# Input tiles by one three-dimensional transfer each, and another order of TensorE's work, in the first two of four image layers

## The chip, the core and the metric

The program runs on one core of one Trainium2 chip. The metric is the device time of one execution in microseconds (us), as the median of several runs. A profile of one execution is shown beside it: TensorE (PE, with its weight loads as PEld), VectorE (DVE), ScalarE (ACT), GpSimd (POOL), and SyncE (SP), which only issues transfers here. A "q" behind an engine's name stands for its queue of issued transfers and of semaphore work.

## What is computed

Sixteen images of 224 x 224 pixels with 32 channels pass four layers. Each adds a function of its group-normalised input to the input. Only layers 0 and 1 are touched by the change:

```python
# layer 0: a shift by an offset that the image's own mean decides
mean_feat = jnp.mean(x, axis=(1, 2))
offsets = jnp.clip(mean_feat @ W + b, 0, 28).astype(jnp.int32)      # dy, dx
x = x + shifted(group_norm(x), dy, dx)                              # zeros come in at the top and left
# layer 1: a 3x3 convolution of signs
y = conv(sign(group_norm(x)), sum_of_signs(W)) + b.sum(axis=0)
x = x + y
# layers 2 and 3: a low-frequency product in a cosine/Fourier basis, plus x @ W.T + b, then relu, added to x
```

## The kernel before

The program has three phases. The first, `shift_conv_forward`, does layers 0 and 1 and the forward spectrum that layer 2 needs. The later phases (names that begin with B_ and C_) do layers 2 and 3 and are not touched.

**Tiles.** An image lies in SBUF as [128 partitions, 12544]; partition 32 i + c holds channel c of every fourth image row (i = 0 to 3). It comes from DRAM in 16 input tiles of [128, 896] f32, each of which holds 28 pixels of 32 channels (3584 bytes in one piece in DRAM) for 128 image rows. VectorE transposes a tile in blocks of 32 x 32 and so turns rows of pixels into rows of channels. Each image is read twice: once as it is (`load_x`, transposed at L805 in `turn_x` straight into `image`), and once shifted by its offset (`load_shifted`, transposed at L815 in `add_shifted` into `moved`, masked, and added to the image at L830). So 32 tiles are read per image. They pass a ring of four buffers `rin`: SyncE issues tile n only when VectorE has turned tile n - 4 (`tile_turned`).

**A tile's load.** `load` (L355 to L361) makes four transfers, one for each i. Each takes 32 pieces of 3584 bytes, 4 image rows apart, to 32 partitions, and adds 16 to the buffer's semaphore when it has landed; VectorE waits for 64.

**The order of the work** is written out by hand. Each engine runs `body(b, ...)` for b = -1 to 15, and each body has 16 slots s = 0 to 15. Body b does at once the convolution of image b (14 units of two double lines, one in each slot 0 to 13), the shifted add of image b + 1, and the plain load and the sums of image b + 2; in its first slots it also finishes the spectrum of image b - 1. `X_BY` and `S_BY` say which tiles fall in which slot: by slot 4 a body has turned 13 of its 32 tiles, by slot 9 it has turned all plain tiles and 10 shifted ones, and the last shifted one is in slot 12.

**TensorE in a slot:** `conv` (L470 to L477, unit s), two spectrum steps in the first slots (L522, L533), in odd slots from 3 `forward_cols`, called the column product here (L509, eight f32 matmuls, product p = (s - 3) / 2 from 0 to 6), and `turn_back` (L498, the transposition of unit s - 1, which waits for VectorE's L838). ScalarE copies what `turn_back` made (`copy_back`, L612) into one of two buffers `tout`, and waits for the column product that read it before; `turn_back` waits for earlier copies.

**The small products** `statistics` (L436): i = 1 and 2 make the group mean and variance of image b + 2 (slots 12 and 13), i = 4 the mean that centres image b + 1 (slot 13), and i = 3, the offset average, multiplies the normalised mean of image b + 2 with the layer's weights (`wsc`, L780). VectorE waits for the offset average at L783 in slot 15, writes the offsets (L792) and signals `off_ready`. SyncE waits for that (L399) before the first shifted tile of the next body, after two plain tiles; everything else in its queue stands behind. In the kernel before, TensorE makes the offset average of image b + 2 in slot 0 of the next body, behind the first unit of its convolution.

**Stores.** ScalarE's queue stores each finished image to `x2s` in seven pieces of 896 KB (L617), SyncE's the spectrum in eight pieces of 32 KB (L379). At the start SyncE fills a padded copy `xpad` of image 0: 14 stores of zeros with 29 rows each (L351), and one copy of 64 rows (L353).

Of the kernel before, what the change touches and what calls it, by code (L numbers as in the profile page):

```python
# [26 lines left out]
SIZE = 224  # L27
C = 32
P = 128
HR = SIZE // 2  # L30
QG = P // C
# [105 lines left out]
def shift_conv_forward(nc, NB, x, w1, b1, w0, b0, con, statm, xpad, x2s, spec):  # L137
# [4 lines left out]
    with Semaphores(nc) as sems, ctx:  # L142
        def sb(name, shape, dt=f32):
            return ctx.enter_context(nc.sbuf_tensor("A_" + name, shape, dt))

        def sem(name):
            return sems.new("A_" + name)

        CHQ = 28
        TILES = 16  # L150
# [4 lines left out]
        RING = 4  # L155
# [8 lines left out]
        rin = [sb(f"rin{i}", [P, CHQ * C]) for i in range(RING)]  # L164
# [48 lines left out]
        in_full = [sem(f"in_full{i}") for i in range(RING)]  # L213
# [40 lines left out]
        def x_tiles(s):  # L254

            return range(X_BY[s - 1] if s else 0, X_BY[s])

        def s_tiles(s):

            return range(S_BY[s - 1] if s else 0, S_BY[s])  # L260

        def x_at(k):

            s = [k < by for by in X_BY].index(True)
            return k + (S_BY[s - 1] if s else 0)

        def s_at(k, has_x):

            return k + (X_BY[[k < by for by in S_BY].index(True)] if has_x else 0)

        def tile_no(b, at):

            return TILES + 2 * TILES * (b + 1) + at

        def tile_loaded(b, at):

            return 64 * (2 * TILES // RING * b + 3 * TILES // RING + at // RING + 1)

        def stat_tiles(s):

# [28 lines left out]
        def ring_base(b):  # L309

            if isinstance(b, int) and b == 0:
                return 0
            return 36 * b - 8
# [33 lines left out]
        @block.sync  # L347
        def _(sp):
            sp.wait_ge(setup, 1)
            for g in range(SIZE * C // BANK):  # L350
                sp.dma_start(xpad[0:29].rearrange("r q c -> r (q c)")[:, g * BANK:(g + 1) * BANK],  # L351
                             zrow).then_inc(pad_done, 16)
            sp.dma_start(xpad[29:29 + P].rearrange("r q c -> r (q c)"),  # L353
                         x[0, 0:P].rearrange("r q c -> r (q c)")).then_inc(pad_done, 16)

            def load(flat, k, slot):
                rows = flat.rearrange("(l f) c -> l (f c)", l=32)
                for i in range(QG):
                    first = i * SIZE + (k % 8) * CHQ
                    sp.dma_start(rin[slot][32 * i:32 * i + 32, :],  # L360
                                 rows[:, first * C:(first + CHQ) * C]).then_inc(in_full[slot], 16)  # L361

            def load_x(b, k, slot):
                load(x_pix[bass.ds(b * (SIZE * SIZE) + (k // 8) * (QG * SECOND * SIZE), P * SIZE), :], k, slot)

            def load_shifted(b, k, slot, back):
                if isinstance(b, int) and b == 0 and k < 8:
                    load(pad_pix[bass.ds(29 * SIZE - back, P * SIZE), :], k, slot)
                else:
                    load(x_pix[bass.ds(b * (SIZE * SIZE) + (k // 8) * (QG * SECOND * SIZE) - back, P * SIZE), :], k, slot)  # L370

            def store_spec(b):
                sp.wait_ge(spec_sb, b + 1)
                sp.sem_inc(off_seen, 1)
                plane = spec[bass.ds(b, 1)].rearrange("o p f -> (o p) f")
                planes = plane.rearrange("(g e c) (m y) -> g e m c y", g=4, e=2, m=16)
                for e in range(2):
                    for g in range(4):
                        sp.dma_start(planes[g, e],  # L379
                                     specout[64 * e + 16 * g:64 * e + 16 * g + 16, :].rearrange("m (c y) -> m c y", y=MODES)  # L380
                                     ).then_inc(spec_stored, 16)

            for k in range(TILES):
                if k >= RING:
                    sp.wait_ge(tile_turned, k - RING + 1)
                load_x(0, k, k % RING)
            sp.wait_ge(pad_done, 16 * (SIZE * C // BANK + 1))

            def body(b, has_x, has_tail):
                back = None  # L390
                for s in range(SLOTS):
                    for k in x_tiles(s) if has_x else ():
                        sp.wait_ge(tile_turned, tile_no(b, x_at(k)) - RING + 1)
                        sp.sem_inc(off_seen, 1)
                        load_x(b + 2, k, x_at(k) % RING)
                    for k in s_tiles(s):
                        if k == 0:
                            sp.wait_ge(off_ready, b + 2)
                            sp.sem_inc(off_seen, 1)  # L399
                            dy = sp.value_load(offi[0:1, 0:1], min_val=0, max_val=MAXOFF)  # L400
                            dx = sp.value_load(offi[0:1, 1:2], min_val=0, max_val=MAXOFF)
                            back = dy * SIZE + dx
                            sp.sem_inc(off_taken, 1)
                        sp.wait_ge(tile_turned, tile_no(b, s_at(k, has_x)) - RING + 1)
                        sp.sem_inc(off_seen, 1)
                        load_shifted(b + 1, k, s_at(k, has_x) % RING, back)
                    if has_tail and s == 6:
                        store_spec(b - 1)

            body(-1, True, False)  # L410
            body(0, True, False)
            with sp.Fori(0, (NB - 4) // 3) as i:
                for k in range(3):
                    body(3 * i + 1 + k, True, True)
            body(NB - 3, True, True)
            body(NB - 2, False, True)
            store_spec(NB - 2)
            store_spec(NB - 1)
            sp.wait_ge(spec_stored, 8 * 16 * NB)

        @block.tensor
        def _(pe):
# [16 lines left out]
            def statistics(b, i):  # L439
                k = average_no(b, i)  # L440
                done = b if i == 4 else b - 1
                if not isinstance(done, int) or done > 0:
                    pe.wait_ge(spec_sb, done)
                if i == 1:
                    average(k, [(mps[:, 2:3], con["k_pair"][:], mv[:, 0:1]), (mps[:, 3:4], con["k_same"][:], mv[:, 0:1])])
                elif i == 2:
                    average(k, [(mps[:, 4:5], con["k_pair"][:], sm[:, 2:3])])
                elif i == 3:
                    average(k, [(mps[:, 6:8], ones[0:C, :], wsc[:])])
                else:  # L450
                    average(k, [(mps[:, 8:9], con["k_pair"][:], sm[:, 8:9])])
# [94 lines left out]
            def body(b, q, has_v, has_s, has_x, has_tail):  # L546
                for s in range(SLOTS):
                    if has_v and s < UNITS:
                        conv(b, s)
                    if has_v and has_s and s == 0:  # L550
                        statistics(b, 3)
                    if has_tail and s < 5:
                        spectrum(b - 1, 2 * s, ring_base(b))
                    if has_v and s >= 3 and s % 2 == 1:
                        forward_cols(b, q, (s - 3) // 2)
                    if has_v and 1 <= s <= UNITS:
                        turn_back(b, q, s - 1)
                    if has_tail and s < 4:
                        spectrum(b - 1, 2 * s + 1, ring_base(b))
                    if has_x and s in (12, 13):  # L560
                        statistics(b + 1, s - 11)
                    if has_s and s == 13:
                        statistics(b, 4)

            body(-1, 2, False, True, True, False)
            body(0, 0, True, True, True, False)
# [137 lines left out]
        def _(dve):  # L704
            at = {"base": 0, "n": 0}
# [26 lines left out]
            for i in range(QG):  # L732
                rows = slice(32 * i, 32 * i + 32)
# [68 lines left out]
            def turn_x(q, k, slot, loaded):  # L802
                t, ch = divmod(k, 8)
                dve.wait_ge(in_full[slot], loaded)
                nc.vector.transpose(turned_view(image[q], SECOND * t, ch * CHQ, CHQ),  # L805
                                    flat_view(rin[slot][:, :])).then_inc(tile_turned, 1)
# [75 lines left out]
            for k in range(TILES):  # L882
                if k >= 8:
                    dve.wait_ge(junk_done, junk_x(0, ("square", k - 8)) + 1)
                turn_x(0, k, k % RING, 64 * (k // RING + 1))
                if k == 0:
                    guess(0, 0)
            for i in (0, 1, 2, 4, 3):
# [958 lines left out]
```

## Time and profile before

| | us |
|---|---|
| median of 3 runs | 3735.57 (3716.77 to 3765.04) |
| the profiled execution's device time | 3730.91 |
| its span, first to last instruction | 3729.1 |
| TensorE busy | 3021.7 (81%) |
| VectorE busy | 2734.8 (73%) |
| ScalarE busy | 1510.7 (41%) |
| DMA, mean over the span | 217 GB/s |

The profile is of one execution. A busy share is a mean over stages with different limits, so the stretches of the first phase are read apart below. "Idle before" is the idle time of an engine just before an instruction, and the name behind the arrow is what ended it. The DMA share is the mean busy share of the core's 16 DMA engines.

### The profile page before, as it was taken

Reading aid. Unit: us, or ns where it says so; the run is one execution under the profiler, and the core shown is the slowest. Engines: PE = TensorE matmul, PEld = TensorE weight load, DVE = VectorE, ACT = ScalarE, POOL = GpSimd, SP = SyncE. Lnnn points to the kernel's source line nnn. Section 1 sums busy time; section 2 is a strip of 40 time slices with the busy share of each in tenths; the row PEclk is TensorE's granted clock in tenths of the full one; section 3 lists DMA queues with packets and bytes.
Section 4 is the critical chain, followed back from the end, with each engine's and each line's share of the span. In section 5 each row is a group of like instructions: output and inputs, shape, how many; then the busy total and the mean of one; then the engine's idle time right before and its main releaser. Section 6 shows DMA issues by size and latency. Waiting matters only on the chain. (4 is left out here: it accounts for less than half of the span.)

```text
span 3729.1 us, 58608 instructions
## 1 busy us (share of the span) xinstructions
PE 3021.7 (81%) x17264; PEld 1399.1 (38%) x17264; DVE 2734.8 (73%) x3908; ACT 1510.7 (41%) x2728; POOL 38.0 (1%) x35
## 2 busy tenths in 40 slices
PE   0188888888888888898937988888898827999997
PEld 0033343333444334344426433333333306444443
DVE  3888777778787777887523677776867643999998
ACT  3466765566665566665443322222222223000000
POOL 0000000000000000000010000000000010000000
PEclk9988887788787778889976999999999867999998
DMA  4677655667565666665364746556465355999998
GB/s 147 174 219 213 199 183 170 192 196 216 175 192 180 190 197 201 195 194 166 122 142 144 287 197 241 227 214 256 186 261 205 144 118 149 341 389 392 377 382 302
DMA packets 272198, 808.67 MB, mean 217 GB/s; under 512 B 85466, under 2 KB 119774, under 8 KB 261108
## 3 DMA queue, kind: packets, MB, share of 16 engines
q1 hardware_dynamic: 212948, 488.15, 41.2%
q10 hardware_dynamic: 58368, 316.72, 21.9%
q8 instruction: 115, 1.88, 0.2%
q0 software_dynamic: 608, 0.63, 0.1%
q14 instruction: 159, 1.30, 0.1%
HBM read 479.39 MB, written 329.56 MB: 217 GB/s over the span
## 5 line engine op out<-in xcount | busy, mean ns | idle before, releaser
L1425 ACT ACTIVATE B_junk<-B_im,B_nk 128x896 bf16<-128x896 f32 x224 | 232.8, 1039 | 718.0 <-DVE B_im L1483 583.2
L470 PE MATMUL A_cps<-A_sign,A_cfull 128*128 128x448 bf16 x1344 | 421.9, 399 | 12.2 <-issue 8.9
L1676 PE MATMUL C_ring<-C_im,C_wnorm 128*128 128x448 f32 x896 | 387.7, 571 | 23.2 <-DVE C_ubuf L1733 17.7
L498 PE MATMUL A_aps<-a_k_ident,A_image 128*112 128x128 f32 x1792 | 289.0, 308 | 134.3 <-DVE A_image L838 112.4
L1371 PE MATMUL B_ring<-B_im,B_wnorm 128*128 128x448 f32 x896 | 385.1, 571 | 7.0 <-DVE B_wnorm L1454 4.8
L612 ACT ACTIVATE A_tout<-A_aps 112x512 f32<-112x512 f32 x448 | 248.3, 591 | 350.1 <-PE A_aps L498 349.6
L475 PE MATMUL A_cps<-A_sign,A_cedge 32*32 32x448 bf16 x1344 | 379.7, 392 | 0.0
L477 PE MATMUL A_cps<-A_sign,A_cedge 32*32 32x448 bf16 x1344 | 379.2, 392 | 0.2 <-issue 0.2
L1343 PE MATMUL B_ring<-B_rout,b_k_rowf 128*64 128x512 f32 x896 | 279.4, 707 | 118.4 <-DVE B_rout L1476 118.4
L838 DVE SCALAR_TENSOR_TENSOR A_image<-A_cps,A_cbias,A_image 128x896 f32<-128x896 f32 x224 | 256.7, 1146 | 156.6 <-PE A_cps L470 153.3
L1483 DVE SCALAR_TENSOR_TENSOR B_im<-B_ring,B_im 128x896 f32<-128x896 f32 x224 | 239.0, 1084 | 175.4 <-PE B_ring L1381 173.8
L815 DVE STREAM_TRANSPOSE A_moved<-A_rin 128x896 f32<-128x896 f32 x256 | 283.3, 1107 | 86.9 <-DMA A_rin<-in_x 71.5
L805 DVE STREAM_TRANSPOSE A_image<-A_rin 128x896 f32<-128x896 f32 x256 | 276.9, 1100 | 88.4 <-DMA A_rin<-in_x 72.2
L498 PEld LDWEIGHTS A_aps<-a_k_ident,A_image 128*112 128x112 f32 x1792 | 239.0, 187 | 254.5 <-issue 189.4
L509 PE MATMUL A_vps<-A_tout,a_k_dctj 112*32 112x512 f32 x896 | 263.4, 717 | 14.9 <-ACT A_tout L612 14.7
L830 DVE SCALAR_TENSOR_TENSOR A_image<-A_moved,A_lin,A_image 128x896 f32<-128x896 f32 (+1 forms) x256 | 265.0, 1035 | 9.1
L1742 DVE STREAM_TRANSPOSE C_rout<-C_im 128x2048 f32<-128x2048 f32 (+1 forms) x128 | 259.2, 2027 | 4.8 <-DMA out<-C_rout 3.2
L1476 DVE STREAM_TRANSPOSE B_rout<-B_im 128x2048 f32<-128x2048 f32 (+1 forms) x128 | 256.5, 2025 | 0.0
L594 ACT ACTIVATE A_junk<-A_image 128x896 bf16<-128x896 f32 (+1 forms) x256 | 219.6, 858 | 79.5 <-DVE A_image L805 69.1
L1371 PEld LDWEIGHTS B_ring<-B_im,B_wnorm 128*128 128x128 f32 x896 | 160.5, 189 | 236.2 <-issue 209.7
L600 ACT ACTIVATE A_junk<-A_image,A_nx 128x896 bf16<-128x896 f32 (+1 forms) x256 | 242.9, 949 | 8.5
L1748 DVE SCALAR_TENSOR_TENSOR C_im<-C_ring,C_im 128x896 f32<-128x896 f32 x224 | 235.0, 1069 | 14.6 <-PE C_ring L1686 12.6
(196 smaller groups left out, 3472.1 us busy)
## 6 DMA issues: line engine op xcount, KB each, us to landing
A_rin<-in_x SPq DMA_DIRECT2D x2016, 112.0 KB, 2.4
x2s<-A_image ACTq DMA_DIRECT2D x112, 896.0 KB, 4.8
B_im<-x2s SPq DMA_DIRECT2D x112, 896.0 KB, 9.6
x3s<-B_im ACTq DMA_DIRECT2D x112, 896.0 KB
C_im<-x3s SPq DMA_DIRECT2D x112, 896.0 KB, 11.9
out<-C_rout ACTq DMA_DIRECT2D x192, 256.0 KB
out<-C_rout ACTq DMA_DIRECT2D x192, 192.0 KB
out<-C_rout ACTq DMA_DIRECT2D x64, 128.0 KB
```

The source lines that it names most:

```text
L470: return nc.tensor.matmul(banks[:, s, 0:LPN], cfull[:, tap, :], lines(n, s, slice(0, P), 0, tap), start=(tap == 0), stop=(tap == 2), skip_ ...
L475: nc.tensor.matmul(banks[bottom, s_top, 0:LPN], cedge[top, tap, :], lines(n, s_top, top, -1, tap), start=False, stop=False, skip_group_che ...
L477: nc.tensor.matmul(banks[top, s_bottom, 0:LPN], cedge[bottom, tap, :], lines(n, s_bottom, bottom, 1, tap), start=False, stop=False, skip_g ...
L498: last = nc.tensor.transpose(aps[side][0:HR, l * P:(l + 1) * P], image[q][:, first:first + 2 * HR].rearrange("p (j s) -> p s j", s=2)[:, l ...
L509: last = nc.tensor.matmul(vps[32 * g:32 * g + 32, :], con["k_dctj"][:, half, :], tout[G % OUTS][:, half, :], start=(half == 0), stop=(half ...
L805: nc.vector.transpose(turned_view(image[q], SECOND * t, ch * CHQ, CHQ), flat_view(rin[slot][:, :])).then_inc(tile_turned, 1)
L815: nc.vector.transpose(moved[:, :].rearrange("p (l q s) -> p q l s", q=CHQ, s=2), flat_view(rin[at_tile % RING][:, :])).then_inc(tile_turne ...
L830: nc.vector.scalar_tensor_tensor(out=dst, in0=m[:, lo:16, :], scalar=lin[:, 0:1], in1=dst, op0=ALU.mult, op1=ALU.add, accum_out=addsum[:, ...
L1343: last = nc.tensor.matmul(bank[64 * side:64 * side + 64, hq, :], con["k_rowf"][:, t, :], rout[p % 2][:, t, q0:q0 + BANK], start=(t == 0), ...
L1371: nc.tensor.matmul(slot(par, ("add", e))[:, lane % 2, 0:2 * SIZE], wnorm[par][:], im[par][:, EVN * e:EVN * (e + 1)].rearrange("p (m s) -> ...
L1676: nc.tensor.matmul(slot(add_place(e))[:, lane % 2, 0:2 * SIZE], wnorm[par][:], im[par][:, EVN * e:EVN * (e + 1)].rearrange("p (m s) -> p s ...
L1742: nc.vector.transpose(flat_view(rout[p][:, 0:wide * C]), turned_view(im[par], SECOND * t, p * PIECEQ, wide)).then_inc(rout_full, 1)
```

## The change

Three edits, all in `shift_conv_forward`:

1. `load` makes one transfer for a tile. Its source is three-dimensional (4 by 32 by 896 elements: i outermost, then the 32 groups of four image rows, then the piece of 3584 bytes), its destination the 128 partitions. The same 128 pieces go to the same places. VectorE waits for 16 where it waited for 64.
2. In slot 13 column product 5 stands behind `turn_back` and the variance product, in place of ahead of them. Column product 6 stays in slot 15; the other five stay too.
3. The offset average of the image after next stands at the end of slot 15, ahead of the next body's first convolution, where it stood behind it.

```diff
         def tile_loaded(b, at):
 
-            return 64 * (2 * TILES // RING * b + 3 * TILES // RING + at // RING + 1)
+            return 16 * (2 * TILES // RING * b + 3 * TILES // RING + at // RING + 1)
...
             def load(flat, k, slot):
-                rows = flat.rearrange("(l f) c -> l (f c)", l=32)
-                for i in range(QG):
-                    first = i * SIZE + (k % 8) * CHQ
-                    sp.dma_start(rin[slot][32 * i:32 * i + 32, :],
-                                 rows[:, first * C:(first + CHQ) * C]).then_inc(in_full[slot], 16)
+                rows = flat.rearrange("(l i q) c -> i l (q c)", i=QG, q=SIZE)
+                first = (k % 8) * CHQ
+                sp.dma_start(rin[slot][:, :], rows[:, :, first * C:(first + CHQ) * C]).then_inc(in_full[slot], 16)
...
                 for s in range(SLOTS):
                     if has_v and s < UNITS:
                         conv(b, s)
-                    if has_v and has_s and s == 0:
-                        statistics(b, 3)
                     if has_tail and s < 5:
                         spectrum(b - 1, 2 * s, ring_base(b))
-                    if has_v and s >= 3 and s % 2 == 1:
+                    if has_v and s in (3, 5, 7, 9, 11):
                         forward_cols(b, q, (s - 3) // 2)
...
                     if has_x and s in (12, 13):
                         statistics(b + 1, s - 11)
+                    if has_v and s == 13:
+                        forward_cols(b, q, 5)
                     if has_s and s == 13:
                         statistics(b, 4)
+                    if has_v and s == 15:
+                        forward_cols(b, q, 6)
+                    if has_x and s == 15:
+                        statistics(b + 1, 3)
...
-                turn_x(0, k, k % RING, 64 * (k // RING + 1))
+                turn_x(0, k, k % RING, 16 * (k // RING + 1))
```

SyncE's instructions at the start of the program, before the change (L360 is the tile's load; a row shows the destination's shape):

```order
L351 DMA xpad<-A_image 29x512 x14
L353 DMA xpad<-in_x 64x14336
L360 DMA A_rin<-in_x 32x896 x72
L400 TENSOR_LOAD A_offi
L400 ISA x2
```

The same place with the change, where the load is L359:

```order
L351 DMA xpad<-A_image 29x512 x14
L353 DMA xpad<-in_x 64x14336
L359 DMA A_rin<-in_x 128x1x896 x18
L398 TENSOR_LOAD A_offi
L398 ISA x2
```

Where 72 transfers loaded 18 tiles, there are 18 now, each with 128 destination rows; their source pattern begins with the dimension of 4.

TensorE in slots 13 and 14 of a body in the loop, before the change, from column product 5 on (L509 column product, L498 `turn_back`, L436 small products; REGISTER_ALU rows only count for waits):

```order
L505 REGISTER_ALU
L509 MATMUL A_vps<-A_tout,a_k_dctj 32x512 x4
L491 REGISTER_ALU
L430 REGISTER_ALU
L498 MATMUL A_aps<-a_k_ident,A_image 112x128 x8
L434 REGISTER_ALU
L436 MATMUL A_wps<-A_sm,a_k_pair 128x1
L434 REGISTER_ALU
L436 MATMUL A_wps<-A_sm,a_k_pair 128x1
L491 REGISTER_ALU
L430 REGISTER_ALU
```

The same place with the change (all lines of TensorE's body are two lower):

```order
L489 REGISTER_ALU
L428 REGISTER_ALU
L496 MATMUL A_aps<-a_k_ident,A_image 112x128 x4
L428 REGISTER_ALU
L496 MATMUL A_aps<-a_k_ident,A_image 112x128 x4
L432 REGISTER_ALU
L434 MATMUL A_wps<-A_sm,a_k_pair 128x1
L507 MATMUL A_vps<-A_tout,a_k_dctj 32x512 x4
L432 REGISTER_ALU
L434 MATMUL A_wps<-A_sm,a_k_pair 128x1
```

The column product moved from ahead of `turn_back` to between the two small products.

TensorE at the seam of two bodies, before the change: the last rows of the next body's first convolution, and the offset average (A_wsc) behind them:

```order
L477 MATMUL A_cps<-A_sign,A_cedge 32x448
L470 MATMUL A_cps<-A_sign,A_cfull 128x448 x2
L434 REGISTER_ALU
L436 MATMUL A_wps<-A_wsc,A_ones 128x2
L430 ISA
L522 MATMUL A_aps<-a_k_ident,A_rowspec 64x128 x4
```

With the change it stands between column product 6 and that convolution:

```order
L502 REGISTER_ALU
L503 REGISTER_ALU
L507 MATMUL A_vps<-A_tout,a_k_dctj 32x512 x4
L432 REGISTER_ALU
L434 MATMUL A_wps<-A_wsc,A_ones 128x2
L463 ISA
L468 MATMUL A_cps<-A_sign,A_cfull 128x448 x2
```

The offset average moved ahead by one unit of the convolution.

## Rows read from the trace of the kernel before

**Rows 1.** Stretches: each engine's busy us (instructions), granted clock, DMA share, GB/s.

```profile
36.00:80.00 44.00, 0.00 (x0) 0.00 (x0) 15.65 (x16) 21.65 (x41) 0.00 (x0) 1.00 0.80 251
170.00:1725.00 1555.00, 1343.78 (x7292) 603.45 (x7292) 1220.77 (x2236) 998.68 (x1898) 0.00 (x0) 0.82 0.63 193
1725.00:1910.00 185.00, 168.68 (x1108) 84.01 (x1108) 89.83 (x171) 78.24 (x146) 0.00 (x0) 0.97 0.35 114
850.00:862.00 12.00, 12.00 (x48) 5.89 (x50) 8.51 (x19) 7.52 (x14) 0.00 (x0) 0.51 0.75 238
870.00:882.00 12.00, 12.00 (x84) 5.79 (x83) 11.22 (x15) 11.84 (x23) 0.00 (x0) 1.00 0.60 192
```

**Rows 2.** Line L783: ns min/median/max, first and last start; whom it waited for.

```profile
L783 DVE TENSOR_TENSOR A_sm<-A_wps,A_b0s x16: 158/159/160, 96.8 to 1723.7; 128x2 f32<-128x2 f32 x16
  PE A_wps L436: 68.7, 16
```

**Rows 3.** Waits from 100 to 1725 us: total us, times, longest.

```profile
PE A_aps L498 <- DVE A_image L838: 111.5, 55, 6.0
DVE A_moved L815 <- DMA A_rin<-in_x: 65.3, 79, 2.6
PE A_wps L436 <- DVEq L845: 47.9, 13, 4.0
...
DVE A_image L805 <- DMA A_rin<-in_x: 41.3, 37, 2.2
```

**Rows 4.** SyncE's queue in order of time: start, us, issues, count.

```profile
2.01 0.43 SPq L132 DMA_DIRECT2D a_k_ident<-k_ident  x1
...
7.07 24.90 SPq L351 DMA_DIRECT2D xpad<-A_image  x14
32.01 3.81 SPq L353 DMA_DIRECT2D xpad<-in_x  x1
...
664.49 39.49 SPq L360 DMA_DIRECT2D A_rin<-in_x  x64
```

**Rows 5.** Stretches of the zero stores: granted clock, DMA share, GB/s.

```profile
20.00:24.00 4.00, 1.00 0.07 26
24.00:28.00 4.00, 1.00 0.07 26
```

**Rows 6.** DMA view, 3300 to 3600 us: packets, MB, then each queue's share.

```profile
DMA packets 21974, 115.26 MB, mean 384 GB/s; under 512 B 5080, under 2 KB 5080, under 8 KB 16039
q1 hardware_dynamic: 10118, 58.58, 49.9%
q10 hardware_dynamic: 11856, 56.68, 46.0%
```

**Rows 7.** DMA view, 60 to 80 us, where only input tiles are loaded.

```profile
DMA packets 2018, 4.84 MB, mean 242 GB/s; under 512 B 670, under 2 KB 670, under 8 KB 2017
q1 hardware_dynamic: 2017, 4.83, 82.6%
A_rin<-in_x SPq DMA_DIRECT2D x44, 112.0 KB, 2.7
```

**Rows 8.** DMA view, 100 to 1800 us: the stores' queue, and issues.

```profile
q10 hardware_dynamic: 14976, 95.43, 14.9%
...
x2s<-A_image ACTq DMA_DIRECT2D x104, 896.0 KB, 4.8
```

**Rows 9.** In order of time, VectorE and TensorE at the end of one body.

```profile
819.27 1.11 DVE L815 STREAM_TRANSPOSE A_moved<-A_rin 128x896 f32<-128x896 f32 x1
...
832.74 0.16 DVE L783 TENSOR_TENSOR A_sm<-A_wps,A_b0s 128x2 f32<-128x2 f32 x1 [3.42 <-PE A_wps L436]
...
814.42 1.91 PE L509 MATMUL A_vps<-A_tout,a_k_dctj 112*32 112x512 f32 x8
...
817.43 0.28 PE L436 MATMUL A_wps<-A_sm,a_k_pair 128*128 128x1 f32 x2
821.66 0.59 PE L436 MATMUL A_wps<-A_sm,a_k_pair 128*128 128x1 f32 x2 [3.95 <-DVEq L845]
823.07 1.96 PE L498 MATMUL A_aps<-a_k_ident,A_image 128*112 128x128 f32 x8 [0.82 <-DVE A_image L838]
825.72 3.63 PE L509 MATMUL A_vps<-A_tout,a_k_dctj 112*32 112x512 f32 x8 [0.69 <-ACT A_tout L612]
```

## The prediction, made before the changed kernel ran

> **What bounds the kernel now.** The change touches only the first phase, so I looked for its period first. The offset line L783 runs once per body; its 16 starts span 96.8 to 1723.7 us [rows 2], so 15 bodies take 1626.9 us, 108.5 us each. Next I read the stretches [rows 1]. From 170 to 1725 us (14.33 bodies) TensorE is busy 1343.8 us, 93.7 per body, VectorE 1220.8 us, 85.2 per body. The DMA engines are busy 63%. So TensorE is nearest to being the bound, with 14.8 us idle per body, at a mean clock of 0.82: some stretches are granted 1.2 GHz (0.51 from 850 to 862 us), others 2.4 GHz (1.00 from 870 to 882), and the instruction counts there, 48 against 84, show that the same work takes 1.75 times as long. The waits [rows 3] say why it idles: 111.5 us for VectorE's L838, 47.9 us for the centring sum at L845. VectorE is late in turn because it waits for tiles, 65.3 + 41.3 = 106.6 us or 7.1 per body, and 68.7 us for the offset average, 4.6 per body [rows 2]. SyncE issues almost without pause: 64 transfers, which are 16 tiles, in 39.5 us, 2.47 us per tile [rows 4]. A body needs a tile every 3.4 us, but after the offset wait they are wanted faster. That is what one transfer per tile addresses.
>
> **The tile's transfer.** It takes three of four issues away, 96 per body. An issue of a 128-row transfer took 0.43 us [rows 4]; four now take 2.47 us. Even if the new one took the 1.78 us of the slowest kind (24.90 / 14) [rows 4], the issue would be cheaper. It isn't the issue that decides, but over how many of the 16 DMA engines the transfer is spread.
>
> Two kinds of rows bear on that. Transfers of 32 and 128 rows load many engines: tiles alone come at 242 GB/s with 82.6% of 16 engines busy [rows 7]. The 14 zero stores of 29 rows do not: while they queue up, the DMA share is 0.07 and the rate 26 GB/s [rows 5], so one engine in 16 (0.0625) works and 15 stand idle. They didn't spread one to an engine either: each is 29 x 2048 = 59,392 bytes, 2.3 us at 26 GB/s, and SyncE issued one every 1.78 us, so two engines would often have been busy at once. So a transfer is dealt out by its outermost dimension, only in equal parts (29 has none), and each starts on the same engine. The new transfer's destination begins with 128 and its source with 4. Equal parts of both exist for 4 engines, not for 16. No transfer in this trace has two sides with different outermost dimensions, so this step is an inference.
>
> The Trainium skill (DMA: Bandwidth & Descriptors, "Why a DMA increments its semaphore by 16 and not by 1") states it outright: the number of engines is the largest up to 16 that divides the slowest dimension of both sides, and these are the lowest-numbered ones. The trace agrees for 29 rows (share 0.07); for 4 against 128 it has no case.
>
> I take 4 engines, always the same 4. A tile is 458,752 bytes. Bounds for one busy engine: 26 GB/s [rows 5]; 384 / (16 x 0.959) = 25.0 in the last phase [rows 6]; and 242 / (16 x 0.826) = 18.3 for today's tiles, whose transfers leave an engine two pieces each [rows 7]. The new transfer leaves 32 pieces in a row on an engine, which is most like the first two, so I take 25.5 GB/s: 458,752 / (4 x 25.5) = 4.5 us per tile. The other end is 6.3 us.
>
> Per body these four engines carry:
> - 32 tiles x 4.5 = 144 us
> - their sixteenth of the image's stores: 14.9% of 1700 us for 104 stores is 2.44 us per store [rows 8], x 7 = 17 us
> - the spectrum's eight 32 KB stores, 16 KB for an engine: under 1 us, left out
>
> That makes 161 us, against 108.5 for the whole body now. The load becomes the bound.
>
> Two things come on top. First, no shifted tile can be issued before the offset is known. From the last tile's transposition at 819.3 to L783 at 832.7 are 13.4 us, of which 3.4 are the wait that edit 3 removes [rows 9]; two plain tiles (9 us) may be issued meanwhile, and the ring restarts with a landing time of some 2.7 us [rows 7]. I take 4 us per body. Second, TensorE's idle time grows from 14.8 to about 60 us per body, and stretches after its waits are granted 1.2 GHz. All its work at that clock would be about 140 us (93.7, of which 36% is slow already: 60 + 33.7 / 1.75 = 79 at full speed, x 1.75 = 139), still under 161. But work and tiles are not spread alike: slots 0 to 4 hold nine spectrum steps and only 13 tiles (58 us). At the low clock TensorE is the later one there. I take 3 us more. A body: 168 us.
>
> **The moved products** cost TensorE nothing in instructions. Edit 3 lets L783 start up to 4.6 us earlier [rows 2]; edit 2 puts column product 5 (eight L509 in 1.91 us at the high clock, 3.63 at the low one) into the 3.95 us in which TensorE waits for the centring sum [rows 9]. Its price: ScalarE's copy of unit 12 waits for this product, and so comes one `turn_back` and one small product later, 1 to 3 us. The next `turn_back` waits for VectorE until 823.1 us anyway [rows 9], so that is hidden. Both gains are worth up to 8 us per body if TensorE or VectorE is the bound, and nothing beyond the 3.4 us already counted if the tiles are.
>
> **The sum.** Bodies 0 to 13: 14 x 168 = 2352. Body -1 has no convolution and no stores: 144 + 6 = 150. Together 2502, against 1627: +875. The first 16 tiles take 44 us now [rows 1]; they become 16 x 4.5 = 72 plus 10 us for their share of the 7.3 MB of the copy to `xpad` ahead of them: +38. Body 14 loads 16 tiles, 72 + 17 us, against some 75 now: +12. The rest (last image, layers 2 and 3) has no tile in it: 0. In all +925. The profiled execution took 3730.9 us, 5 us under the median, so 3730 + 925 = 4655 us.
>
> **Rivals.**
> - *The transfer spreads over all 16 engines.* For it: the destination has 128 rows, like loads that do spread. Then most of the tile waits (7.1 per body) and of the offset wait (4.6) go; VectorE and TensorE lean on each other, so I count half: 6 us x 15 = 90, and 5 in the prologue: 3640 us, faster. It decides against my forecast as soon as a tile takes under (108.5 - 17) / 32 = 2.86 us, which is from 7 engines up. Beside it stands another rule of the Trainium skill (DMA: Bandwidth & Descriptors, "Rules for kernel authors"): many small transfers are better coalesced, and two to separate partitions are better made one of 128 partitions. Chance 0.10.
> - *Four engines, but other ones for each tile.* Then a tile lands some 6.5 us after its issue, which a ring of four, 3.4 us a tile, mostly hides; only the first tiles after the offset come late, 4 us, which eats the gain: about 3700 us, no change. Against it: the zero stores stayed on one engine. Chance 0.05.
> - *The same four, at 18.3 GB/s each.* If pieces of 3584 bytes are slow by themselves, a tile takes 6.3 us: 32 x 6.3 + 17 + 5 = 224 per body; 14 x 224 + 207 - 1627 = +1716, with +80 at both ends about 5525 us. Chance 0.07.
> - *Forecast as worked out.* Chance 0.78.
>
> **How the numbers follow.** The low end leaves out what I put on top and lets half of the stores pass beside the tiles: 14 x 153 + 144 = 2286, +659, and +40: about 4430; a little room below gives 4400. The high end takes TensorE late in the first five slots and a rate midway to the rival's (5.1 us a tile): 14 x 188 + 170 = 2802, +1175, and +70: about 4975; 5080 with room. It leaves out both fast cases (0.15) and most of the slow one. A change over 2% is about what these runs can tell: faster 0.09, same 0.05 (with a little of the first rival), slower 0.86.
>
> **What would show it.** Right: in the first phase the DMA share falls to about 0.25 plus the stores' part, the rate to some 110 to 130 GB/s; VectorE's waits for A_rin grow from 107 to over 700 us; TensorE's clock falls below 0.82; a tile's time to landing, with others queued ahead, is over 9 us; L783's 16 starts span about 2500 us. Wrong: a rate of 200 GB/s or more in that phase, or tiles landing in 3 us. L783's own wait should be nearly gone in any case.

## The result, and the profile after

| | before | with the change |
|---|---|---|
| median us | 3727.28 (4 runs) | 4640.93 (4 runs, 4636.58 to 4660.22) |
| span of the profiled execution, us | 3729.1 | 4634.8 |
| ratio | | 1.244, 95% interval 1.234 to 1.254 |

The change makes the kernel 24% slower. The forecast was 4655 us, the range 4400 to 5080. All ratios in this text are to runs of the kernel before made beside the run in question (medians 3725 to 3732 us for the experiments).

Where the time went is seen from the first transfer of the second phase in SyncE's queue. Before (start, us, issue):

```profile
1910.48 0.38 SPq L132 DMA_DIRECT2D b_k_pair<-k_pair  x1
```

With the change:

```profile
2818.78 0.37 SPq L132 DMA_DIRECT2D b_k_pair<-k_pair  x1
```

The first phase takes 908.3 us longer, the whole span 905.7. So all of it is in the phase that loads tiles.

Its period is that of the offset line, now L785 (ns min/median/max, first and last start, and below it the wait):

```profile
L785 DVE TENSOR_TENSOR A_sm<-A_wps,A_b0s x16: 151/159/161, 132.8 to 2599.4; 128x2 f32<-128x2 f32 x16
  PE A_wps L434: 7.3, 13
```

Fifteen bodies take 2466.6 us, 164.4 each, against 108.5 [rows 2]. The first of them, body -1, has no convolution and is shorter: it took 147.9 us (the second start is at 280.7), so the fourteen full bodies took 165.6 each. VectorE's wait for the offset average has nearly gone, 7.3 us for 68.7. The same stretch, with each engine's busy us, the clock, the DMA share and GB/s, and the last image behind it:

```profile
133.00:2599.00 2466.00, 1637.67 (x7277) 717.36 (x7278) 1303.87 (x2332) 1050.06 (x1963) 0.00 (x0) 0.68 0.32 128
2600.00:2785.00 185.00, 165.87 (x991) 77.60 (x990) 88.53 (x164) 67.66 (x127) 0.00 (x0) 0.87 0.27 103
```

TensorE is busy 66% of the stretch instead of 86% [rows 1], and longer for the same work, since the granted clock is 0.68 for 0.82. The DMA share is halved, 0.32 for 0.63, and that is the point: as a group the DMA engines look two thirds idle while everything waits for them. The waits of this stretch (total us, times, longest):

```profile
DVE A_moved L817 <- DMA A_rin<-in_x: 685.3, 232, 6.3
...
PE A_aps L496 <- DVE A_image L840: 577.5, 140, 12.2
DVE A_image L807 <- DMA A_rin<-in_x: 364.2, 181, 5.3
...
ACT A_tout L614 <- PE A_vps L507: 146.6, 14, 11.0
```

VectorE waits for tiles 1049.5 us, where it was 106.6 [rows 3], nearly every tile of the 480 (413 times), and TensorE waits for VectorE. The DMA view of the stretch says on how many engines the tiles run:

```profile
DMA packets 105668, 314.60 MB, mean 128 GB/s; under 512 B 31768, under 2 KB 31768, under 8 KB 105496
## 3 DMA queue, kind: packets, MB, share of 16 engines
q1 hardware_dynamic: 91384, 222.71, 23.0%
q10 hardware_dynamic: 14112, 89.92, 9.0%
```

The tiles' queue (q1) keeps 0.23 x 16 = 3.7 engines busy. The stores (q10) use 9% of all 16. If q1 is on four engines only, these are busy 92% of the time with tiles and 9% with stores, which leaves next to nothing. (It comes to 101%, so the times of packets of the two queues must overlap in part.) Two short stretches of one body, between two stores, show the same: while tiles come, the DMA share is 0.25, and around the offset nearly nothing moves (us, each engine's busy us, clock, DMA share, GB/s):

```profile
1440.00:1444.00 4.00, 3.27 (x12) 0.65 (x14) 1.34 (x8) 0.58 (x1) 0.00 (x0) 0.50 0.07 14
1446.00:1448.00 2.00, 1.14 (x6) 0.67 (x5) 1.93 (x5) 0.59 (x1) 0.00 (x0) 0.50 0.25 95
```

VectorE's tile transpositions show the rhythm (start, us, then idle time before):

```profile
1404.49 1.12 DVE L817 STREAM_TRANSPOSE A_moved<-A_rin 128x896 f32<-128x896 f32 x1 [1.21 <-DMA A_rin<-in_x]
1408.86 1.11 DVE L817 STREAM_TRANSPOSE A_moved<-A_rin 128x896 f32<-128x896 f32 x1 [2.29 <-DMA A_rin<-in_x]
1413.37 1.11 DVE L817 STREAM_TRANSPOSE A_moved<-A_rin 128x896 f32<-128x896 f32 x1 [0.33 <-DMA A_rin<-in_x]
1417.61 1.11 DVE L817 STREAM_TRANSPOSE A_moved<-A_rin 128x896 f32<-128x896 f32 x1 [2.16 <-DMA A_rin<-in_x]
1424.13 1.11 DVE L817 STREAM_TRANSPOSE A_moved<-A_rin 128x896 f32<-128x896 f32 x1 [2.85 <-DMA A_rin<-in_x]
1428.49 1.11 DVE L817 STREAM_TRANSPOSE A_moved<-A_rin 128x896 f32<-128x896 f32 x1 [2.29 <-DMA A_rin<-in_x]
...
1451.31 1.11 DVE L817 STREAM_TRANSPOSE A_moved<-A_rin 128x896 f32<-128x896 f32 x1 [2.48 <-DMA A_rin<-in_x]
```

A tile comes every 4.36 us (4.24 to 4.51 here), however long VectorE had idled: 458,752 bytes in 4.36 us is 105 GB/s, or 26.3 for each of four engines. Once it is 6.5 us (1417.6 to 1424.1). ScalarE issued a store at 1414.34, and the 2.2 us more are what its sixteenth, 57,344 bytes, takes at 26.3 GB/s. The last two rows are the last shifted tile of one body and the first of the next; between them stand two plain tiles, which had landed by then, and the offset.

### The profile page after: what moved, and what is told of

It reads as the page before. It is cut to its first block and busy times, and to the rows that moved or that the text cites. A ratio compares the mean times of both kernels' runs of the same rounds, so it can differ in the third digit from the quotient of the medians.

```text
span 4634.8 us, 54387 instructions
## 1 busy us (share of the span) xinstructions
PE 3326.3 (72%) x17264; PEld 1516.8 (33%) x17264; DVE 2757.5 (59%) x3908; ACT 1529.8 (33%) x2728; POOL 38.0 (1%) x35
## 5 line engine op out<-in xcount | busy, mean ns | idle before, releaser
L496 PE MATMUL A_aps<-a_k_ident,A_image 128*112 128x128 f32 x1792 | 382.3, 379 | 605.7 <-DVE A_image L840 588.2
L614 ACT ACTIVATE A_tout<-A_aps 112x512 f32<-112x512 f32 x448 | 259.2, 594 | 1053.7 <-PE A_aps L496 891.7
L496 PEld LDWEIGHTS A_aps<-a_k_ident,A_image 128*112 128x112 f32 x1792 | 304.8, 200 | 748.4 <-issue 589.3
L468 PE MATMUL A_cps<-A_sign,A_cfull 128*128 128x448 bf16 x1344 | 502.8, 466 | 5.1 <-issue 5.0
L473 PE MATMUL A_cps<-A_sign,A_cedge 32*32 32x448 bf16 x1344 | 458.3, 460 | 0.0
L475 PE MATMUL A_cps<-A_sign,A_cedge 32*32 32x448 bf16 x1344 | 457.5, 460 | 0.0
L1678 PE MATMUL C_ring<-C_im,C_wnorm 128*128 128x448 f32 x896 | 388.1, 572 | 25.7 <-DVE C_ubuf L1735 20.7
L507 PE MATMUL A_vps<-A_tout,a_k_dctj 112*32 112x512 f32 x896 | 296.6, 798 | 12.4 <-ACT A_tout L614 12.4
```

The lines of the kernel that those rows point to most:

```text
L468: return nc.tensor.matmul(banks[:, s, 0:LPN], cfull[:, tap, :], lines(n, s, slice(0, P), 0, tap), start=(tap == 0), stop=(tap == 2), skip_ ...
L473: nc.tensor.matmul(banks[bottom, s_top, 0:LPN], cedge[top, tap, :], lines(n, s_top, top, -1, tap), start=False, stop=False, skip_group_che ...
L475: nc.tensor.matmul(banks[top, s_bottom, 0:LPN], cedge[bottom, tap, :], lines(n, s_bottom, bottom, 1, tap), start=False, stop=False, skip_g ...
L496: last = nc.tensor.transpose(aps[side][0:HR, l * P:(l + 1) * P], image[q][:, first:first + 2 * HR].rearrange("p (j s) -> p s j", s=2)[:, l ...
L507: last = nc.tensor.matmul(vps[32 * g:32 * g + 32, :], con["k_dctj"][:, half, :], tout[G % OUTS][:, half, :], start=(half == 0), stop=(half ...
L1678: nc.tensor.matmul(slot(add_place(e))[:, lane % 2, 0:2 * SIZE], wnorm[par][:], im[par][:, EVN * e:EVN * (e + 1)].rearrange("p (m s) -> p s ...
```

## The experiments

The first question was whether the engines are counted by the outermost dimension. The load of the changed kernel reads `(l i q) c -> i l (q c)` with i = 4. With another number in its place the transfer is of the same kind and size, and only its outermost dimension changes.

**16 outermost.**

```diff
-                rows = flat.rearrange("(l i q) c -> i l (q c)", i=QG, q=SIZE)
+                rows = flat.rearrange("(l i q) c -> i l (q c)", i=16, q=SIZE)
```

> The changed kernel, with the source of each tile's one transfer read as 16 by 8 by 896 elements in place of 4 by 32 by 896: still one three-dimensional transfer of 128 pieces of 3584 bytes to 128 partitions, but its rows land on other partitions, so that the image is computed with its rows permuted. My theory (a transfer is dealt over as many engines as divide the outermost dimension of both sides, here 16): the load is no longer the bound, the DMA share in the first phase goes back to 0.6 or more, the 16 starts of the offset line span under 1600 us and the time is about 3640 us (3550 to 3720). Rival (a three-dimensional or a single transfer is slow as such, whatever its dimensions): about 4640 us, as the changed kernel.

Measured: 3670.7 us, ratio to before 0.982 (0.975 to 0.988). The 900 us are gone, and a little more; the DMA share from 170 to 1725 us is 0.71, and the 16 starts of the offset line span 1561 us. The DMA view from 200 to 1700 us:

```profile
q1 hardware_dynamic: 91894, 206.06, 54.6%
```

That is 8.7 engines' worth of packet time at a time, which four engines can't give. A single three-dimensional transfer is not slow as such.

**8 outermost**, the same edit with `i=8`.

> The same with 8 by 16 by 896 elements, again with the rows permuted. My theory: 8 engines, 2.25 us a tile, 32 x 2.25 + 17 = 89 us of load per body, under the 108.5 us that a body took before: about 3670 us (3600 to 3760), near the run with 16. Rival (slow as such): about 4640 us. If the time went with the reciprocal of the engines without a floor, it would be some 4000 us.

Measured: 3817.2 us, ratio 1.024 (1.019 to 1.029). It is far from 4640, as it should be, but not hidden: I expected 3670. The DMA view from 200 to 1700 us, and the offset line:

```profile
q1 hardware_dynamic: 82233, 192.46, 38.7%
q10 hardware_dynamic: 13104, 83.50, 14.0%
```

```profile
L785 DVE TENSOR_TENSOR A_sm<-A_wps,A_b0s x16: 151/159/161, 99.6 to 1804.8; 128x2 f32<-128x2 f32 x16
```

q1 moved 192.46 MB in 1500 us with 0.387 x 16 = 6.2 engines busy, 20.7 GB/s for a busy one, not 25.5. So a tile takes 458,752 / (8 x 20.7) = 2.8 us: 32 of them are 89 us, with stores 106, and with some 10 us around the offset (below) 116. The fifteen bodies took 113.7 us on average, the fourteen full ones 115.7 (the second start is at 184.6). At today's 108.5 us per body 8 engines are just too few.

**2 outermost**, the same edit with `i=2`.

> The changed kernel with the source of each tile's transfer read as 2 by 64 by 896 elements (rows permuted, as in the runs with 8 and 16). My theory: 2 engines. In the changed kernel four engines took 4.8 us of packet time each per tile (23.0% of 16 engines over 2400 us for 461 tiles), so two take 9.6 us: 32 x 9.6 + 17 + 4 = 328 us per body, and 3730 + (14 x 328 + 312 - 1627) + some 200 at both ends is about 7200 us (6800 to 7600). Rival (four engines whatever the dimension is, or a loss that does not grow with fewer engines): 4640 us.

Measured: 6780.9 us, ratio 1.819 (1.810 to 1.827). The DMA view from 200 to 1700 us:

```profile
q1 hardware_dynamic: 27736, 75.63, 12.5%
```

0.125 x 16 = 2.0: two engines, busy all the time. The time is 19 us under the range that I gave, because I took 9.6 us for a tile. Its transposition starts, where no store comes between, are 8.7 us apart:

```profile
1317.20 1.11 DVE L817 STREAM_TRANSPOSE A_moved<-A_rin 128x896 f32<-128x896 f32 x1 [5.59 <-DMA A_rin<-in_x]
1325.93 1.11 DVE L817 STREAM_TRANSPOSE A_moved<-A_rin 128x896 f32<-128x896 f32 x1 [6.66 <-DMA A_rin<-in_x]
```

That is twice the 4.36 us of four engines. 32 x 8.73 + 17 = 296 us, and the bodies took 296.9 on average ((4657.8 - 203.6) / 15) for the 328 that I had expected.

**Four transfers, each with 4 outermost.** The runs so far all have one transfer. This one has four, as the kernel before, and TensorE's new order:

```diff
 # against the kernel before; TensorE's new order is there too
-                rows = flat.rearrange("(l f) c -> l (f c)", l=32)
+                rows = flat.rearrange("(m a f) c -> a m (f c)", a=4, m=8)
...
-                                 rows[:, first * C:(first + CHQ) * C]).then_inc(in_full[slot], 16)
+                                 rows[:, :, first * C:(first + CHQ) * C]).then_inc(in_full[slot], 16)
```

> Four transfers for each tile, 32 rows each, as before the change, with TensorE's new order; but the source of each is read as 4 by 8 by 896 elements, so that its outermost dimension is 4 (rows permuted within each group of 32 partitions). My theory: each of the four runs on the same four engines, and the tile is as slow as one transfer of 4 by 32: about 4650 us (4550 to 4800). Rival (it is the single transfer with one semaphore count, or its 128 rows, that is slow): 3743 us, as with four plain transfers.

Measured: 4658.3 us, ratio 1.249 (1.244 to 1.255), with this DMA view from 200 to 1700 us:

```profile
q1 hardware_dynamic: 59293, 135.56, 23.1%
```

Four transfers on four engines are as slow as one on four, and these four tile transfers run on the same engines, or there would be more than 3.7 busy. The loss does not come from making one transfer of four. What counts is the source's outermost dimension, though the destination's is 32. In all these runs the smaller of the two sides divides the larger one; that equal parts of both are what is needed, and not the smaller side, has only the zero stores of 29 rows to show for it [rows 5], where both sides are 29.

The second question was what the moved products do.

**The load alone** (edit 1, TensorE's order of before).

```diff
 # against the changed kernel
+                    if has_v and has_s and s == 0:
+                        statistics(b, 3)
...
-                    if has_x and s == 15:
-                        statistics(b + 1, 3)
```

Column product 5 is back in its old place too.

> The kernel before with edit 1 alone: one transfer of 4 by 32 by 896 for each tile, TensorE's order as before. My theory: the load alone makes the loss, and the offset average is back behind the first convolution, so that the offset comes 3 to 5 us later in each of 15 bodies: about 4690 us (4640 to 4750). Rival (the moved products take a good part of the loss, since ScalarE waits for column product 5 in the changed kernel): 4400 us or less.

Measured: 4715.8 us, ratio 1.267 (1.261 to 1.273). It is 75 us slower than the whole change: with slow tiles the new order is worth 5 us per body. VectorE's wait at its offset line is back, 72.8 us for 7.3, 4.4 per body:

```profile
  PE A_wps L434: 72.8, 16
```

**The load and the offset average, without edit 2.**

```diff
 # against the changed kernel
-                    if has_v and s in (3, 5, 7, 9, 11):
+                    if has_v and s >= 3 and s % 2 == 1 and s < 15:
...
-                    if has_v and s == 13:
-                        forward_cols(b, q, 5)
```

> The changed kernel without edit 2: one transfer of 4 by 32 by 896 for each tile and the offset average ahead of the first convolution, but column product 5 back ahead of the transposition. My theory: all of the 75 us between the changed kernel (4641) and the load alone (4716) come from edit 3, since the offset gates the shifted tiles: 4640 us (4620 to 4665). Rival (edit 2 brings them): 4716 us.

Measured: 4647.3 us (4637.7 to 4654.7), ratio 1.246. That is the changed kernel's time. So edit 3 brings the 75 us, and edit 2 nothing measurable, with slow tiles.

**The order alone** (edits 2 and 3, four plain transfers).

```diff
 # against the kernel before
-                    if has_v and has_s and s == 0:
-                        statistics(b, 3)
...
+                    if has_v and s == 13:
+                        forward_cols(b, q, 5)
...
+                    if has_x and s == 15:
+                        statistics(b + 1, 3)
```

> The kernel before with edits 2 and 3 alone: four transfers for each tile, TensorE's new order. My theory: VectorE's wait for the offset average (4.6 us a body) goes and half of it reaches the end, some 3 us in 15 bodies, and the centring wait hides column product 5: about 3670 us (3620 to 3710). Rival (ScalarE's copy of unit 12 comes later and takes the gain back): 3720 to 3760 us, no change.

Measured: 3742.7 us, ratio 1.004 (1.001 to 1.006): no gain, but a loss of 0.4%. My theory said 3670 and falls; the rival's time is right, and its reason is not borne out by the one body looked at below. The waits of this kernel from 100 to 1725 us:

```profile
DVE A_image L842 <- PE A_cps L470: 163.6, 44, 6.8
ACT A_tout L616 <- PE A_vps L509: 109.1, 14, 9.5
```

and VectorE's wait at its offset line:

```profile
  PE A_wps L436: 3.8, 8
```

For the kernel before, the same view has this row:

```profile
DVE A_image L838 <- PE A_cps L470: 94.9, 30, 6.7
```

The offset wait fell by 64.9 us, and the wait for the convolution grew by 68.7. VectorE gets past the offset earlier and then stands before the next convolution, which TensorE reaches no sooner. So the offset wait was a place where VectorE waited for TensorE's pace, not what made the pace. ScalarE's wait for column product 5 looks large, 109.1 us, but it mostly takes the place of a wait for the transposition (294.5 us in the kernel before, 179.8 here). In one body the transposition of unit 12 ended at 823.2 us and the copy began at 825.24, 2 us later, behind the product; what comes next, the transposition of unit 13, began at 828.71 because of VectorE:

```profile
825.24 1.08 ACT L616 ACTIVATE A_tout<-A_aps 112x512 f32<-112x512 f32 x2 [5.15 <-PE A_vps L509]
```

```profile
828.71 1.13 PE L498 MATMUL A_aps<-a_k_ident,A_image 128*112 128x128 f32 x8 [1.03 <-DVE A_image L842]
```

**16 outermost with the old order.** Perhaps the offset counts once tiles are fast.

> One transfer of 16 by 8 by 896 for each tile (rows permuted), with TensorE's order of the kernel before. It tells what edits 2 and 3 are worth when tiles are fast. With the new order the same load took 3671 us. Theory (TensorE is the bound, and VectorE's wait for the offset average only becomes a wait for the convolution, as in the run of the order alone): within 0.5% of that, 3655 to 3690 us. Rival (with the tile waits gone the offset's time counts in full, 4.6 us in 15 bodies): 3735 us.

Measured: 3666.1 us, ratio 0.984 (0.979 to 0.989), against 3670.7 and 0.982 with the new order. It does not: VectorE's waits change places here too (67.6 us at the offset line and 86.0 for the convolution with the old order, 5.8 and 165.6 with the new one). The order is worth 5 us per body when tiles are late, and nothing when TensorE is.

**A better kernel?** The runs with 16 put the image's rows on other partitions, so they are no version. They gained 55 and 66 us, and in the first of them VectorE's waits for tiles from `in_x` had fallen to 47.0 us (31.9 + 15.1, 100 to 1725 us) from 106.6. GpSimd's queue was idle, so it can take half of the issues and leave the rows alone:

```diff
 # the plain tiles' transfers leave SyncE's queue; in GpSimd's:
+            def body(b):
+                for k in range(TILES):
+                    pool.wait_ge(tile_turned, tile_no(b, x_at(k)) - RING + 1)
+                    load_x(b + 2, k, x_at(k) % RING, pool, in_x)
...
```

The plain tiles get semaphores of their own (`in_x`).

> A candidate: edits 2 and 3, four transfers of 32 rows per tile as before, but the 16 plain tiles of a body are issued from GpSimd's queue, which was idle, and SyncE issues the shifted ones. My theory (SyncE's issue of 2.47 us per tile makes VectorE's tile waits, and the spread over 16 engines is kept): the tile waits mostly go, about 3670 us (3620 to 3710), as in the run with 16. Rival (GpSimd's issue costs more per transfer than SyncE's, and its tiles come later): 3740 us or more.

Measured: 3698.2 us (10 runs), ratio 0.992 (0.988 to 0.995). That is 27 us, half of what I had expected.

> The candidate with plain tiles issued from GpSimd's queue, but TensorE's order of the kernel before. Theory (the order is worth nothing on either side of it): 3698 us, as with the new order (3680 to 3715). Rival (the new order costs the 0.4% that it cost alone): 3683 us.

Measured: 3691.9 us (12 runs), ratio 0.989 (0.985 to 0.993). With and without the new order the intervals overlap. Of the three comparisons of the two orders with tiles on 16 engines only the first, of the order alone, is clear of noise; where its 0.4% come from was not found. This is the fastest version with rows in place, by 1.1%. Its tile waits from 100 to 1725 us:

```profile
DVE A_moved L821 <- DMA A_rin<-in_x: 70.1, 46, 4.0
...
DVE A_image L811 <- DMA A_rin<-in_x: 24.5, 24, 2.4
```

The plain tiles' waits fell from 41.3 to 24.5 us, but those for shifted tiles, which SyncE still issues, did not (65.3 before). So SyncE's issue, which my theory blamed, does not seem to make most of the tile waits. The DMA view from 500 to 1500 us has a tile's transfers landing later than before (KB, median us from issue to landing), first this kernel:

```profile
A_rin<-in_x POOLq DMA_DIRECT2D x609, 112.0 KB, 3.2
A_rin<-in_x SPq DMA_DIRECT2D x600, 112.0 KB, 3.4
```

and the kernel before:

```profile
A_rin<-in_x SPq DMA_DIRECT2D x1142, 112.0 KB, 2.4
```

Only 12 us of the 40 that the median fell are in the tile waits. VectorE's waits for the offset average and for the convolution fell too, 68.0 to 51.9 and 94.9 to 75.7 us; what made them fall was not settled.

## Why the prediction was right

**The number of engines.** The step that decided, that equal parts of both outermost dimensions are dealt over the engines and that they are the same ones each time, was an inference from the zero stores [rows 5]. It holds as far as it was tested: shares of 12.5%, 23.0% and 23.1% are two engines and nearly four of 16, for outermost dimensions of 2, 4 and 4. That it is the largest count of equal parts, and not simply the smaller of the two sides, stays an inference for tiles, since no run tells these apart. The rule of the Trainium skill that the prediction names (DMA: Bandwidth & Descriptors, "Why a DMA increments its semaphore by 16 and not by 1") says the same, and these runs agree with it, also where the two sides differ (4 against 128, 4 against 32).

**The sum, term by term, per body.** It came to 168 us for a full body, and 165.6 were measured; for body -1 it came to 150, and 147.9 were measured.
- A tile: 4.5 us forecast, 4.36 seen, so 139.5 for 144. The rate of [rows 5] and [rows 6] was the right one to take, not that of [rows 7].
- Stores: 17 us forecast; 9.0% of 2466 us for 98 stores are 2.3 us for one, 16 for seven.
- Around the offset: 4 us forecast. From the last shifted tile (1428.5) to the first of the next body (1451.3) are 22.8 us, and three tiles would have taken 13.1, so 9.7; over fourteen such places the mean is 8.8. Mis-sized. The steps up to the offset line took 10.6 us for the 10.0 counted. Not counted were the 3.4 us from that line (1439.12) to SyncE's issue (1442.50). From the issue to the tile's transposition were 8.8 us, 4.4 more than the tile's own time, where I had put 2.7. That edit 3 is worth 5 us a body here fits: nothing hides this chain.
- The low clock in slots 0 to 4: 3 us forecast, about 0 seen. The clock did fall, from 0.82 to 0.68, but in the shade of the tiles: in the trace the tiles' packets pause for some 7 us a body at the offset, once more for about 1.1 us, and nowhere else for over 0.3 us. So in the loop the tiles never waited for TensorE or VectorE.

As seen, the terms add up to 139.5 + 16 + 8.8 = 164.3. There were two errors of some 5 us each, with opposite signs, and two smaller ones. That the total is off by only 2.4 us is in part luck; that the tiles bound the body is not.

The rows of the offset line and of SyncE's next issue (x5 is five issues with what lies between them):

```profile
1439.12 0.16 DVE L785 TENSOR_TENSOR A_sm<-A_wps,A_b0s 128x2 f32<-128x2 f32 x1 [0.58 <-PE A_wps L434]
1442.50 10.73 SPq L359 DMA_DIRECT2D A_rin<-in_x  x5
```

**The ends.** The prologue took 132.8 - 96.8 = 36 us more, forecast 38. Behind the fifteenth body 30 us more were lost in the span, forecast 12. Body 14, the last to load tiles, lost them. From the last offset line to the last tile's transposition (1795.3 before, 2703.9 now) it took 104.5 us for 71.6, 33 more; I had put 89 for 75. From there to the second phase's first transfer are 114.9 us, before 115.1. The 33 us lie in three places. The first tile came 10.9 us behind the offset line for 8.2, the next six took 41.1 us for 33.8, and the last nine 52.5 for 29.7. Only the last nine wait for tiles. For the second to the seventh VectorE waited for no tile; the granted clock from 2600 to 2704 us is 0.81, where it was 1.00 from 1724 to 1796. So the low clock that I had charged to the bodies of the loop seems to have cost some 7 us here, where fewer tiles are loaded; no run separates it.

**The moved products.** Under slow tiles the forecast counted edit 3 only as 3.4 us less of the offset's chain; alone it is worth 5 us per body. For the case of fast tiles I had said "up to 8 us per body if TensorE or VectorE is the bound". That is wrong, as the order alone shows: no gain. I had added a wait that VectorE has for TensorE to what TensorE's idle time could give back. The hidden price of edit 2, 1 to 3 us on ScalarE, was 2 us in the one body looked at, and hidden there.

**The rivals.** Spread over 16 engines, 3640 us: the run with 16 took 3670.7, so its price was nearly right, and what speaks against it is now shown. Its turning point was not: I put it at 2.86 us a tile, from 7 engines up, and 8 still lose 2.4%. Two terms were missing, the fall of an engine's rate when more of them work, and the 10 us around the offset: (108.5 - 17 - 10) / 32 = 2.5 us, where 8 engines need 2.8. Other engines for each tile: excluded by the run of four transfers with 4 outermost. The rate of 18.3 GB/s: excluded by the 4.36 us.

**What was to be seen.** The DMA share of 0.25 plus the stores' part was 0.32; the rate 128 GB/s (110 to 130 said); tile waits over 700 us were 1049.5; the clock under 0.82 was 0.68; L783's own wait, now L785's, is nearly gone; the starts span 2466.6 us (2500 said). A tile's time to landing is not given by the profile of the changed kernel, so that sign could not be read.

## What to carry to other kernels

Before merging transfers, look at the outermost dimension of both sides: in these runs it decided how many DMA engines worked, and one small dimension in front undid what the merge saved. A DMA share that stays low while an engine waits for transfers is the sign; multiply the share of the queue that is waited for by 16 and look for a small whole number (here 2.0 and 3.7). And a wait of one engine for another is no gain to be had if the other one sets the pace: find what stands behind the wait before counting it.

## What the runs showed of the hardware

**The rate of an engine.** By the pace of the tiles, an engine moved 26.3 GB/s with four at work (458,752 bytes in 4.36 us) and 26.3 with two (in 8.73 us), and one alone 26 [rows 5]. With more of them it moved less. Where the pace is not set by tiles alone, q1's MB over its packets' time gives a rate that can be compared: 25.2 GB/s with 2, 24.5 with 4 (222.71 MB / (0.230 x 16 x 2466 us)), 20.7 with 8, and 15.7 with 16 (206.06 MB / (0.546 x 16 x 1500 us)). It lies under the pace, presumably because packets that overlap in time are counted twice, and its step from 2 to 4 is not in the pace. What slows 8 and 16 was not tested; the pieces are of 3584 bytes in each.

**The issue of a transfer** is not a fixed price. SyncE's rows for the tiles' transfers (ns min/median/max), with the change:

```profile
L359 SPq DMA_DIRECT2D A_rin<-in_x x504: 528/553/10575, 35.7 to 2685.6; - x168
```

and with 2 outermost:

```profile
L359 SPq DMA_DIRECT2D A_rin<-in_x x504: 523/8274/14931, 36.0 to 4788.6; - x168
```

The same instruction takes 0.55 us where four engines carry it, and 8.3 us where two do, which is nearly the 8.73 us in which these move a tile. With the change only the third and fourth of these issues took over 2.7 us, namely 5.2 and 10.6, soon behind the copy of 3584 KB to `xpad`. So a slow issue can be a queue that drains slowly, and no sign that the issuing engine is the bound. But a row of many issues in the queue's timeline is not the time of its issues:

```profile
35.73 81.13 SPq L359 DMA_DIRECT2D A_rin<-in_x  x18
```

Of these 81.1 us (with the change), 46.9 are SyncE's waits for VectorE to free a buffer of the ring:

```profile
SPq L359 <- DVE A_image L807: 46.9, 12, 4.7
```

So too with the 39.5 us for 64 transfers from which I worked out 2.47 us per tile [rows 4]: in the kernel before, the issue itself takes 0.316 us at the median, 20 us for 64, and the rest is work on registers between them and a few longer issues.
